# TensorE's three small-product stages run whole instead of in halves, between projections of six

## What is computed

```python
def step(S, inp):
    rk_t, wk_t, v_t, g_t, b_t = inp
    pred = jnp.einsum('bhk,bhkd->bhd', wk_t, S)
    err = (v_t - pred) * b_t[..., None]
    S = S + wk_t[..., None] * err[..., None, :]
    o = jnp.einsum('bhk,bhkd->bhd', rk_t, S) * g_t[..., None]
    return (S, o)
```

## Time and profile before

| | us |
|---|---|
| median of 3 runs | 2510.26 (2506.84 to 2511.02) |
| the profiled execution | 2514.57 |
| span of the profile | 2512.8 |
| PE busy in the span | 2150.4 (86%) |
| DVE busy | 2056.9 (82%) |
| POOL busy | 1936.0 (77%) |
| ACT busy | 1739.4 (69%) |

### The profile page before, as it was taken

The page is one execution under the profiler, slowest core; times in us unless marked ns, Lnnn a source line. Parts: engine busy times, 40 slices in busy tenths (PEclk is TensorE's granted clock), DMA queues, the critical chain, the costliest instruction groups (busy, mean ns, idle before and its releaser), DMA issues. The chain is left out here.

```text
span 2512.8 us, 146586 instructions
## 1 busy us (share of the span) xinstructions
PE 2150.4 (86%) x61989; PEld 1350.3 (54%) x61989; DVE 2056.9 (82%) x5963; ACT 1739.4 (69%) x3500; POOL 1936.0 (77%) x3224
## 2 busy tenths in 40 slices
PE   1679999999999999998999999999998747787775
PEld 1356666566565666665666566666665523344442
DVE  4487998899888899988889898888998637777874
ACT  3767878777787778877887787778874335555554
POOL 1667888888788888888888888888886326777777
PEclk7789999999999999999999999999999768888888
DMA  2112222222222222222222222222222134556554
GB/s 81 50 43 59 80 75 79 77 74 75 71 80 76 75 73 80 80 72 75 80 77 73 74 80 78 74 76 80 77 63 69 46 128 124 153 152 165 151 135 100
DMA packets 132134, 215.47 MB, mean 86 GB/s; under 512 B 31352, under 2 KB 31360, under 8 KB 131488
## 3 DMA queue, kind: packets, MB, share of 16 engines
q1 hardware_dynamic: 131488, 206.20, 28.4%
HBM read 104.40 MB, written 67.11 MB: 68 GB/s over the span
## 5 line engine op out<-in xcount | busy, mean ns | idle before, releaser
L757 DVE TENSOR_TENSOR ps_elim<-ps_elim,sys 128x30 f32<-128x30 f32 (+14 forms) x1920 | 543.4, 326 | 0.8
L765 DVE TENSOR_TENSOR sys<-sys,ps_elim 128x30 f32<-128x30 f32 (+14 forms) x1920 | 534.8, 316 | 1.0
L882 PE MATMUL ps_v<-wv,xt 128*128 128x512 f16 x1536 | 433.6, 392 | 30.4 <-DMA kbd<-kt 17.2
L882 PE MATMUL ps_y<-wo,ot 128*128 128x512 f16 x1536 | 406.5, 388 | 9.5 <-DVE x L809 8.7
L1285 PE MATMUL ps_f<-wq,f_xq 128*128 128x512 f16 x1024 | 280.4, 424 | 103.0 <-ACT f_yn L1161 98.3
L909 PEld LDWEIGHTS ps_chain<-rhs,t_t 32*32 32x32 f32 x16384 | 262.9, 144 | 130.7 <-issue 129.2
L909 PE MATMUL ps_chain<-rhs,t_t 32*32 32x32 f32 x16384 | 294.9, 219 | 22.3 <-issue 16.3
L666 ACT ACTIVATE state<-ps_s 128x512 f32<-128x512 f32 x128 | 76.4, 597 | 268.8 <-PE ps_s L973 268.6
L903 PEld LDWEIGHTS ps_chain<-state,key_t 32*32 32x32 f32 x16384 | 175.2, 106 | 152.5 <-issue 151.6
L973 PEld LDWEIGHTS ps_s<-err,key_b 32*32 32x32 f32 x16384 | 172.7, 107 | 147.1 <-issue 146.7
L903 PE MATMUL ps_chain<-state,key_t 32*32 32x32 f32 x16384 | 211.3, 195 | 39.0 <-issue 38.4
(11 more groups left out here) (153 smaller groups left out, 5260.8 us busy)
## 6 DMA issues: line engine op xcount, KB each, us to landing
x_in<-in_L_attn_x SPq DMA_DIRECT2D x128, 256.0 KB
kbd<-kt SPq DMA_DIRECT2D x512, 64.0 KB
x_res<-in_L_attn_x SPq DMA_DIRECT2D x128, 256.0 KB
x_scratch<-x SPq DMA_DIRECT2D x128, 256.0 KB, 6.4
f_x<-x_scratch SPq DMA_DIRECT2D x32, 1024.0 KB, 7.6
out<-f_res SPq DMA_DIRECT2D x128, 256.0 KB, 3.9
gate<-gates SPq DMA_DIRECT2D x128, 7.9 KB
gate<-gates SPq DMA_DIRECT2D x128, 0.2 KB
```

The source lines that it names most:

```text
L757: dve.tensor_tensor(tmp, factors(r, c, first, end)[:, c - first:C - 1 - first, c - first:c - first + 1].to_broadcast(shape), sys[:, r, c:c ...
L765: dve.tensor_tensor(dst, dst, tmp, ALU.add).then_inc(elim_done[r], 1)
L882: last = pe.matmul(out, lhs[:, a, kb, :], weights[:, w, kb, :], start=(i == 0), stop=(i == 3 * KB - 1))
```

## The change

PE's prediction, error and update are each issued as one run of 64 products. The value projection is cut in two pieces of six, one on either side of the gram products, and the output projection in two pieces of six, one ahead of the update and one at the step's end. Nothing is added or taken away: the same products, the same semaphores and the same waits, in another order. The signal of the value projection (v_psum) moves from between the halves of the error to ahead of it, pred_psum comes three projection products earlier, the wait `error_ready` stands three further on, and `update_ready` three further on.

```diff
-            def blocks(half):
-
-                for h in range(half * H // 2, (half + 1) * H // 2):
+            def blocks():
+
+                for h in range(H):
...
-            SHARE = WHOLE // 4
+            PART = WHOLE // 2
...
-                predict(0)
...
-                value(0, SHARE)
-                last = predict(1)
-                if live:
-                    last.then_inc(s["pred_psum"], 1)
-                value(SHARE, 2 * SHARE - 1)
+                    for h, q, e in blocks():
+                        last = pe.matmul(ps_chain[q, e], key_t[q, l, h, :], state[q, l % 2, e], start=True, stop=True)
+                    last.then_inc(s["pred_psum"], 1)
...
+                    project(ps_v[:, :], xt[:, v_l % 4], k["wv"], range(PART - 1))
                 gram_ready(base, j)
-                value(2 * SHARE - 1, 2 * SHARE)
...
-                value(2 * SHARE, 3 * SHARE - 1)
...
+                    project(ps_v[:, :], xt[:, v_l % 4], k["wv"], range(PART, WHOLE - 1))
                 error_ready(base, j)
-                value(3 * SHARE - 1, 3 * SHARE)
-                solve_error(0)
-                last = value(3 * SHARE, 4 * SHARE)
...
+                    project(ps_v[:, :], xt[:, v_l % 4], k["wv"], range(WHOLE - 1, WHOLE)).then_inc(s["v_psum"], 1)
...
-                output(0, SHARE - 1)
+                    project(ps_y[:, :], ot[:, y_l % 2], k["wo"], range(PART - 1))
                 update_ready(base, j)
-                output(SHARE - 1, SHARE)
-                update(0)
-                output(SHARE, 2 * SHARE)
-                last = update(1)
...
```

More of the change, by code:

```diff
@@ L887, in _ @@
             WHOLE = 3 * KB
-            SHARE = WHOLE // 4
+            PART = WHOLE // 2
             def step(base, j):
                 n, l, live = on(base, j, 0)
-                v, v_l, v_live = on(base, j, LAG_V)
[L894 to L900, removed]
-                    if live:
[L902 to L913, removed]
-                predict(0)
+                if live:
+                    if not on(base, j - 1, LAG_Y)[2]:
+                        chain_ready(base, j)
+                    for h, q, e in blocks():
+                        last = pe.matmul(ps_chain[q, e], key_t[q, l, h, :], state[q, l % 2, e], start=True, stop=True)
+                    last.then_inc(s["pred_psum"], 1)
+                v, v_l, v_live = on(base, j, LAG_V)
                 if v_live:
@@ L929, in step @@
                             out = ps_gram[q, :].rearrange("p (i h) -> p h i", h=H)[:, HB * g:HB * g + HB, :]
-                            last = pe.matmul(out, kt[:, m_l % 2, g, q], kbd[:, m_l % 2, :, g, q], start=True, stop=True)
+                            last = pe.matmul(out, kt[:, l % 2, g, q], kbd[:, l % 2, :, g, q], start=True, stop=True)
                     last.then_inc(s["gram_psum"], 1)
-                value(2 * SHARE, 3 * SHARE - 1)
+                if v_live:
+                    project(ps_v[:, :], xt[:, v_l % 4], k["wv"], range(PART, WHOLE - 1))
                 error_ready(base, j)
-                value(3 * SHARE - 1, 3 * SHARE)
-                solve_error(0)
-                last = value(3 * SHARE, 4 * SHARE)
                 if v_live:
-                    last.then_inc(s["v_psum"], 1)
-                last = solve_error(1)
+                    project(ps_v[:, :], xt[:, v_l % 4], k["wv"], range(WHOLE - 1, WHOLE)).then_inc(s["v_psum"], 1)
+                n, l, live = on(base, j, 0)
                 if live:
+                    for h, q, e in blocks():
+                        last = pe.matmul(ps_chain[q, e], t_t[q, l // 2 % 2, :, l % 2, h], rhs[q, e], start=True, stop=True)
                     last.then_inc(s["err_psum"], 1)
@@ L963, in step @@
                 y, y_l, y_live = on(base, j, LAG_Y)
[L964 to L975, removed]
                 if y_live:
@@ L979, in step @@
                     wait(pe, s["ot_done"], y + 1)
-                output(0, SHARE - 1)
+                    project(ps_y[:, :], ot[:, y_l % 2], k["wo"], range(PART - 1))
                 update_ready(base, j)
-                output(SHARE - 1, SHARE)
-                update(0)
-                output(SHARE, 2 * SHARE)
-                last = update(1)
+                if y_live:
+                    project(ps_y[:, :], ot[:, y_l % 2], k["wo"], range(PART - 1, PART))
+                n, l, live = on(base, j, 0)
                 if live:
+                    for h, q, e in blocks():
+                        last = pe.matmul(ps_s[q, e], key_b[q, l, e], err[q, l % 2, e],
+                                         start=(isinstance(n, int) and n == 0 and h == 0), stop=True, skip_group_check=True)
                     last.then_inc(s["s_psum"], 1)
@@ L1003, in step @@
                     project(ps_g[:, 0:2 * H], xt[:, v_l % 4], k["wgb"], range(WHOLE)).then_inc(s["g_psum"], 1)
[L1005 removed]
                 if y_live:
+                    project(ps_y[:, :], ot[:, y_l % 2], k["wo"], range(PART, WHOLE - 1))
                     chain_ready(base, j + 1)
[L1008 to L1010 removed]
+                    project(ps_y[:, :], ot[:, y_l % 2], k["wo"], range(WHOLE - 1, WHOLE)).then_inc(s["y_psum"], 1)
             run(step)
```

10 lines of the change are left out of this document (4 added, 6 removed).

## The result

The changed kernel takes 2581.78 us (median of 4 runs, 2579.09 to 2590.41) against 2510.64 for the kernel before (2506.84 to 2513.66): a ratio of 1.0297, 95% interval 1.0262 to 1.0333, 71 us slower. The prediction said slower, by 24 us, and 2572 at most. Its sign and its mechanism held; its size did not. Two steps of it failed: the term for the pages, taken as 0.2 us a step where 0.40 was lost, and the lower clock, left out of the sum as a rival, where it added some 20 us.

A forecast was written before the change was run, and what follows sets the result against it. PE's own instruction list, stalling at page fetches, was taken as the bound. Border savings were not credited, waits counted nothing, pages added 0.2 us over 118 steps: 2510 + 24 = 2534 us, range 2500 to 2572.

The forecast's parts named there:

- the term for the pages: Full attention steps: instructions stand closer together, so dense pages wait longer for the next; 0.2 us a step, +24 us.
- the lower clock: Rival: stalls of 2.5 us drop PE to 1.2 GHz, 2.5 us lost in one step of eight; 2571 us, chance 0.12.
- The page: PE's instruction stream: 256 instructions per fetch, each page costing the longer of its running time and its fetch.
- F: Time of one instruction page fetch on PE, about 3.6 to 4.4 us; 3.73 or 3.88 by the sums over page starts.
- eight starts: Sum over pages starting at every 59th MATMUL of a step: F = 3.73, 0.16 us a step more.
- all 472: Same sum with pages starting at every MATMUL of a full step: F = 3.88, 0.34 us a step more.
- PE's stock: Instructions PE holds ahead; if long enough that bunching did not matter, 0 more and the step stays at 14.76 us.
- under 0.98: Granted clock from 200 to 1850 us: falling below this would show the prediction wrong in the slower direction.
- The savings at the borders: Fewer borders between small and large products in full steps: 0.80 us a step off PE's running time, 13.39 to 12.6.
- rival 2: The border saving arrives in full steps while stalls stay or shrink: 94 us won, 2416 us; whole or in part, chance 0.15.
- Rival 1: Only the number of pages counts on PE, so time stays within 0.2%, 2505 to 2515 us; chance 0.13.
- The signs named ahead: Window 200 to 1850 us: steps of 14.9 to 15.0 us, PE busy 0.5 less a step, more issue idle, same packets.
- The waits, priced at nothing: Moved waits and signals of the full steps keep enough cover or come earlier, so they change the time by nothing.

The follow-up runs named there:

- narrow_before: Kernel before with ten of the twelve products of each projection cut to a quarter of their width, same instructions: 2494.8 us, ratio 0.9971.
- inline_late pair: Kernel before and changed order, both with waits riding on products and the gram copy's wait at the first transpose: 2436.10 and 2517.19 us.
- after_again: The changed kernel measured once more, on another chip, against the kernel before: 2605.0 us, ratio 1.0308.
- narrow pair: Kernel before and changed kernel, both with ten products of each projection at a quarter of their width: 2494.75 and 2514.45 us.
- pred_whole: Kernel before with only the prediction made whole, error and update still in halves: 2558.5 us, ratio 1.0118.
- waits_before: Kernel before with three long satisfied semaphore waits added to eleven products of each projection: 2643.4 us, ratio 1.0457.
- inline_late: Kernel before, same product order, waits riding on products or dropped if covered, gram copy's wait left at the first transpose: 2436.10 us, ratio 0.9753.

## Why the prediction was right in its sign and too small

**The page.** Right, and carried by the most evidence: the distances of whole multiples of 256 instructions between pauses in both kernels, one packet for each page, 12 packets for 3058 added instructions, and the 3.90 us a page of narrow_before. That a page costs F on average however little its instructions run is shown. That the fetch of the next page begins only when a page is entered was called an inference; the packets' start times in the trace support it, since after a stall the next packet starts mostly 1.2 to 1.7 us after PE has resumed, takes about 1.15, and PE gets its page about 1.4 after the packet's end, 3.7 to 4.2 together. No experiment tested it by itself.

**The term of the sum that was mis-sized: the pages.** The prediction had 0.16 a step by eight starts, 0.34 by all 472, 0 if PE's stock were long, and took 0.2 "between 0 and 0.34". Undisturbed steps lost 0.40 (14.73 to 15.13), and 0.39 in the inline_late pair. The sum over all starts was the good one; leaning towards a long stock was the error. No softening by a stock is to be seen. Eight starts were too few for stages with borders that sharp: they gave F = 3.73, where narrow_before has 3.90. The missing 0.06 comes out of the lengths below: the sum over all 472 starts, done again with the whole stages as long as the changed kernel shows them (1.36, 1.38 and 1.95 us, and 1.40 for six projections), gives some 0.06 more than with the prediction's 1.22 and 1.38, an estimate. At 0.40 the kernel would have come out 47 us slower, at 2557, the end of the forecast's own range.

**The rival that was no rival.** The clock was treated as a case beside the forecast, with a chance of 0.12, and it came on top of it. PE at the stretch around 1182 us, timeline and then windows:

```profile
1178.78 1.04 PE L897 MATMUL ps_chain<-state,key_t 32*32 32x32 f32 x98
1181.54 0.45 PE L897 MATMUL ps_chain<-state,key_t 32*32 32x32 f32 x30 [1.72 <-issue]
1181.92 2.12 PE L882 MATMUL ps_v<-wv,xt 128*128 128x512 f16 x6
1183.96 1.94 PE L915 MATMUL ps_gram<-kbd,kt 128*32 128x128 f32 x32
```

```profile
1182.60:1186.00 3.40, 3.40 (x37) 1.77 (x36) 3.32 (x12) 2.64 (x7) 3.15 (x6) 0.50 0.24 84
```

After a stall of 1.72 us in the prediction the granted clock is 0.50, the 1.2 GHz level, for 3.4 us, and gram takes 1.94 instead of the 1.08 of the earlier trace rows. There are 11 such stretches from 200 to 1850 us (20 in after_again), where the kernel before has one. Each begins within some 4 us of a pause of over 1.5 us between PE's instructions; but of the 46 pauses of that length 36 have none behind them, so a long pause alone does not tell when the clock falls. Half speed for 3.4 us costs at most 1.7 us, 19 us for the eleven. They touch 12 of 108 steps, which last 16.86 us on average against 15.13: 0.19 a step over all, some 20 us. The forecast had the mechanism, a step in eight, but 2.5 us for a hit where the trace has 1.7. Together: 118 x 0.40 = 47 and 20 make 67 of the 71 us. That the 2571 given to this rival comes within 11 us is partly luck: its 37 us for the clock were about 17 too many, the 24 under them 23 too few. The prediction's own bound, "under 0.98", was not crossed (0.99): eleven short stretches hardly show in a mean.

**The savings at the borders.** Six projection products take 1.40 (1.38 taken). A whole prediction without a gap takes from 1195.05 to 1196.40 here, and a whole update from 1191.54 to 1192.92:

```profile
1191.54 1.42 PE L962 MATMUL ps_s<-err,key_b 32*32 32x32 f32 x128
1192.92 0.61 PE L974 MATMUL ps_gram<-ident_half,o_part 128*128 128x128 f16 x8
...
1195.05 1.42 PE L897 MATMUL ps_chain<-state,key_t 32*32 32x32 f32 x128
1196.40 1.25 PE L882 MATMUL ps_v<-wv,xt 128*128 128x512 f16 x5
```

That is 1.35 and 1.38, not the 1.22 of the earlier trace rows, and what two halves take (0.68 or 0.69 each). Why that one update took 1.22 is not shown. The error made whole takes 1.95, as forecast. The saving was nearer to 0.5 than to 0.80 us a step, and none of it arrived, so rival 2 failed for the reason that the prediction gave against it. The trace agrees with the Trainium skill on the 0.12 us for a merged pair (TensorEngine Tiling (Array Packing), section Key Properties: a change of the tiling mode drains TensorE), but here the rule ranked two kernels the wrong way round. The other page that was weighed (Runtime: NRT & Kernel Launch, section Instruction fetch mechanics) calls the cost of going from one block to the next "mostly hidden"; narrow_before, where the fetch is the pace at 3.90 us a page, does not agree.

**Rival 1, the fetches alone set the pace.** Fell: the packets are 486 in both kernels and the time is not the same. It becomes nearly true where all pages are short, in the narrow pair.

**The signs named ahead.** Seen: PE busy less (1454.83 / 107.8 = 13.50 us a step against 13.86, 0.4 where 0.5 was said), single stalls of 2.6 us inside a run of 128, issue up on prediction and update, the same number of packets. Wrong: the idle time of the error was to rise with the others and went from 7.4 to 6.2 us; stalls on the value projection were to be rarer and went from 11.7 to 27.2 us, since the gap behind a dense page falls on what follows the prediction, as it fell on the gram products at 317.12 above; DVE's wait for the prediction was to rise and fell to 131.7, while its wait for g_den rose from 26.7 to 78.0. Steps of 14.9 to 15.0 were to be seen; it was 15.31.

**The waits, priced at nothing.** Right for the difference: pred_whole is slower though none of the waits that it moves shows idle time, and no wait of PE on another engine appears in the changed kernel. What went unnoticed is that the waits of the kernel before had a price of their own, 0.52 us a step, which the change neither adds nor removes.

**What stays open.** Whether the update made whole really costs more than the others, and why the parts cost more than their sum; and why an instruction that only looks at a semaphore costs 40 to 53 ns when its share of a page is 15. The traces hold a lead. Each such instruction is on record with 51 ns (all 3545 of waits_before in the window), and after a pause of over 0.7 us the next packet starts the later the more of them there are. The median is 1.16 us in inline_late (0.1 a step), 1.34 in the kernel before (10.0) and 1.66 in waits_before (34.0). That fits a fetch which is put off by the time PE's sequencer spends on them; no run tests it by itself.

## What to carry to other kernels

Where an engine shows "issue" gaps that come after the same number of instructions each time, count them and the packets of the instruction queue before the products: its pace is then set by the longer of running time and fetch, page by page, and small instructions are better kept apart by large ones than gathered. In such a kernel remove instructions first, the separate waits above all, by letting each wait ride on the product that needs it, and never put it earlier than its signal comes. When a case of the forecast makes stalls longer, add what the stalls bring with them, here a lower clock, rather than setting it beside the forecast as a rival.

## What the runs showed of the hardware

- Pages of 256 of PE's instructions followed each other by 3.90 us on average in narrow_before where the clock did not fall, though its instructions ran only 2.7 us a page. With hardly a separate semaphore instruction left the mean was 1650 / 428 = 3.86 (inline_late), so this is no fixed number.
- An instruction on PE that only looks at a long satisfied semaphore cost 40 ns (waits_before) to 53 ns (inline_late, by taking them out). Each is on record with 51 ns. What a wait costs that rides on a product was not separated; in inline_late the waits that were kept ride on products, and the kernel gained 62 us all the same.
- The granted clock was 0.50 for 3.4 us behind a stall of 1.7 us in the prediction (the row of 1182.6 us); behind the stall of 2.25 us that ended at 317.12 it stayed at 1.00. narrow_before, with less work and 114.2 us of stalls on the prediction, had a mean of 0.90, and gave part of what it gained back to the clock.
